# Two layers of a diffusion transformer block: the products of the identity ahead of two kinds of transposes are taken out

## The reference

```python
# layer 0
x_norm = modulate(_ln(x), shift_a, scale_a)
...
attn_w = jax.nn.softmax(jnp.einsum('bhqd,bhkd->bhqk', q, k) * scale, axis=-1)
attn_out = jnp.einsum('bhqk,bhkd->bhqd', attn_w, v)
...
x = x + gate_a[:, None] * attn_out
...
x = x + c_attn_out
...
x = x + gate_m[:, None] * h
# layer 1
x = res + sa
...
x = res + ca
...
x = res + (h @ ffn_w2.T + ffn_b2)
```

## Time and profile before

| | |
|---|---|
| time, median of 3 runs | 448.67 us (448.65 to 450.5) |
| profiled execution, from its first to its last instruction | 447.5 us |
| granted TensorE clock, mean over the span | 0.935 |
| PE busy | 399.2 us (89%) |
| DVE busy | 324.1 us (72%) |
| ACT busy | 263.9 us (59%) |
| POOL busy | 157.5 us (35%) |

### The profile page before, as it was taken

One profiled execution on the slowest core, in us unless ns is written; L12 is line 12 of the kernel. 1 busy time (PEld: TensorE's weight loads), 2 busy tenths in 40 slices (PEclk: granted clock), 3 DMA queues, 4 the chain that ended last, 5 costly groups with the idle time before them and its releaser, 6 DMA issues.

```text
span 447.5 us, 11248 instructions
## 1 busy us (share of the span) xinstructions
PE 399.2 (89%) x4368; PEld 256.7 (57%) x4368; DVE 324.1 (72%) x842; ACT 263.9 (59%) x521; POOL 157.5 (35%) x147
## 2 busy tenths in 40 slices
PE   1688989898988899999999999999999999989976
PEld 1445646464656654745646547556665665656754
DVE  6559686969687876794986977987999977381430
ACT  1414847464748585865756756537475667549642
POOL 6793384252615320251321602515526061011220
PEclk9965998969899999998998998969999989989999
DMA  7990030303030321030120120213030303000000
GB/s 233 278 351 7 2 144 3 145 3 140 3 141 3 139 91 51 4 144 3 48 97 4 47 97 4 97 51 115 27 112 30 141 3 139 26 3 4 25 25 23
DMA packets 18059, 33.58 MB, mean 75 GB/s; under 512 B 2527, under 2 KB 7135, under 8 KB 17759
## 3 DMA queue, kind: packets, MB, share of 16 engines
q1 hardware_dynamic: 16992, 28.85, 18.1%
q10 hardware_dynamic: 1015, 4.02, 3.0%
HBM read 6.51 MB, written 1.05 MB: 17 GB/s over the span
## 4 chain that ended last, share of the span: by engine, by line
PE 59%; DVE 22%; ACT 11%; issue 5%; ACTq 1%; DMA 1%; POOL 0%; DVEq 0%
DVE maxima L807 15%; PE ps_ao L1142 12%; PE ps_misc L1073 8%; PE ps_misc L1122 8%; ACT PT L989 7%; PE ps_misc L1171 6%; PE ps_misc L1193 5%; PE ps_misc L1098 4%; PE ps_misc L1022 4%; PE ps_misc L1178 3%; PE ps_misc L1083 3%; PE ps_misc L1027 2%; PE ps_misc L1151 2%; ACT xnT L974 2%; ACT L989 1%
## 5 line engine op out<-in xcount | busy, mean ns | idle before, releaser
L807 DVE TENSOR_REDUCE maxima<-ps_misc 128x4 f32<-128x512 f32 (+1 forms) x256 | 153.1, 663 | 21.9 <-PE ps_misc L1098 21.6
L989 ACT ACTIVATE PT<-ps_misc 128x512 f32<-128x512 f32 (+1 forms) x256 | 131.0, 607 | 30.2 <-PE ps_misc L1122 28.9
L887 POOL TENSOR_SCALAR Kd<-Kh,head_rows 128x512 fp32r<-128x512 f32 (+1 forms) x64 | 98.6, 1558 | 94.5 <-DVE maxima L807 69.5
L1142 PE MATMUL ps_ao<-PT,V 120*18 120x128 f32 (+1 forms) x2048 | 76.6, 296 | 5.1 <-ACT PT L989 4.4
L1142 PEld LDWEIGHTS ps_ao<-PT,V 120*18 120x18 f32 (+1 forms) x2048 | 55.2, 105 | 23.1 <-ACT PT L989 11.3
L1122 PE MATMUL ps_misc<-Qd,Ks 32*128 32x128 f32 (+1 forms) x1024 | 56.3, 293 | 10.0 <-ACT PT L989 4.6
L1122 PEld LDWEIGHTS ps_misc<-Qd,Ks 32*128 32x128 f32 (+1 forms) x1024 | 42.6, 191 | 34.6 <-issue 16.9
L868 POOL TENSOR_SCALAR vareps<-mv 128x4 f32<-128x4 f32 (+1 forms) x28 | 6.8, 243 | 149.9 <-DVE mv L700 149.3
L1098 PE MATMUL ps_misc<-Kd,Qh 32*128 32x512 f32 (+1 forms) x256 | 44.0, 528 | 1.0 <-DVE maxima L807 0.2
L852 DVE TENSOR_TENSOR x<-ps_misc,x 128x512 f32<-128x512 f32 x24 | 16.5, 689 | 38.6 <-PE ps_misc L1193 28.5
L1073 PE MATMUL ps_misc<-xnT,Wr 128*128 128x512 f32 x72 | 39.3, 668 | 4.7 <-ACT xnT L974 4.7
(11 more groups left out here) (80 smaller groups left out, 482.1 us busy)
## 6 DMA issues: line engine op xcount, KB each, us to landing
Qd<-Qh SPq DMA_DIRECT2D x32, 256.0 KB, 2.6
Ks<-Kh SPq DMA_DIRECT2D x16, 256.0 KB, 3.1
Qd<-Ql SPq DMA_DIRECT2D x16, 256.0 KB, 2.5
Ks<-Kh SPq DMA_DIRECT2D x16, 240.0 KB, 2.5
Ks<-Kl SPq DMA_DIRECT2D x8, 256.0 KB, 2.4
Ks<-Kl SPq DMA_DIRECT2D x8, 240.0 KB, 2.5
W<-weights ACTq DMA_DIRECT2D x1, 1792.0 KB, 15.6
x<-x_in SPq DMA_DIRECT2D x4, 256.0 KB, 6.9
```

What stands on the lines that cost most here:

```text
L807: dve.tensor_reduce(maxima[:, st.b // HB, st.b % HB, c, :], bank(st.use + c)[:, 0:NG * ns].rearrange("p (n k) -> p n k", n=NG), AX_X, ALU. ...
L887: pool.tensor_scalar(Kd[:, st.f % 2, st.h, 0:n], f32(Kh[:, st.f % 2, 0:n]), head_rows[:, st.h:st.h + 1], None, ALU.mult).then_inc(S["kd_re ...
L989: act.activation(PT[0:ns, st.k % PSLOTS, c, :, :].rearrange("p n t -> p (n t)"), bank(st.use + c)[0:ns, :], ACT.Exp, scale=SCALE).then_inc ...
L1142: last = pe.matmul(ps_ao[32 * c:32 * c + PAIR, block * P:(block + 1) * P], heads[:, at:at + PAIR], PT[0:ns, st.k % PSLOTS, c, n, :], start ...
```

## The change

The table `WARM` becomes empty, so that `warm` does nothing in any step. The order of all steps, all waits and all other instructions stay.

```diff
@@ -60,7 +60,7 @@
 PAIR = 2 * VW
 VSLOTS = 3
 PSLOTS = 3
-WARM = {"norm": 3, "aT": 3}
+WARM = {}
 
 
 WCOLS = {}
```

## The result

| | before | after |
|---|---|---|
| median | 448.81 us | 456.11 us |
| single runs | 448.65 to 450.5 (4) | 452.06, 455.41, 456.81, 460.4 |
| profiled execution's span | 447.5 us | 453.5 us |
| mean granted clock, profiled execution | 0.935 | 0.906 |

The ratio is 1.0128, 95% interval 1.0088 to 1.0168. The forecast was 453.0 us, 443 to 462, slower.

What follows compares the result with a forecast made beforehand. PE was taken to set the pace in most stages. A gain of 12.5 us and a clock loss of 16.8 us gave +4.3 us, 453.0 us against the median, range 443 to 462 us.

Steps and rivals of the forecast that it cites:

- The price of 1 us at 1.2 GHz: Read from three passes of attention 0: each 3.4 us at 1.2 GHz makes the kernel 1.4 us longer.
- the loss: Ten more clock falls, about 12 lengths of 3.4 us, 41 us more at 1.2 GHz, costing 16.8 us.
- The gain: Removing 48 products gives back 12.5 us, at 22 places on the chain; bounds about 8 and 16.6 us.
- the full places: 13 chain places where the copy has long landed; each gives its whole 0.65 or 0.75 us, 9.05 us together.
- the 22 places: Products on the chain of work that ended last: 13 give all, eight 0.34 to 0.55 us, one nothing.
- The ten places: Ten sparse stretches holding products at 2.4 GHz; without them PE keeps 2.48 us of work, so ten new falls.
- The clock didn't hold: Rival that the clock holds: fewer than seven lengths added, kernel faster, 443 us with five, 436 with none; 23%.
- The products weren't hidden: Rival that products only fill time lost to waits: 448.7 us and the same clock; no more than 2%.
- Transposes do hold the clock: Rival that transposes don't hold the clock: a fall at every second place, 24 lengths, 470 us; 5%.

Runs made afterwards that it cites:

- The kernel with the products off the chain kept: Against the kernel before, only 13 norm and 14 aT products stay, those off the chain or giving nothing; 444.2 to 456.2 us, mean 449.9.
- the quarter products: Against the kernel before, all 48 products keep 384 columns but use 32 rows of the identity in place of 128; 457.5 us.
- the six transposes: Against the kernel before, six transposes of the identity into the same bank replace the product at all 48 places; 448.1 us.
- the experiment with eleven products kept: Against the kernel before, products stay at only 11 of 48 places, those of the prediction's ten sparse stretches; 451.6 us.
- the 16 products of aT alone: Against the kernel before, products stay only ahead of the 16 aT, the 32 ahead of norm are out; 448.6 us.
- the 32 of norm: Against the kernel before, products stay only ahead of the 32 norm, the 16 ahead of aT are out; 452.0 us.

## Why the prediction was right

**The direction and the mechanism held.** Low clock went from 55.0 us in the mean of 79 runs to 92.3 us in four, 37 us more; the forecast was 41. (In the two profiled executions it is 34 us behind the first norm, and 27 us in all.) The price of 1 us at 1.2 GHz was set at 1.4 / 3.41 = 0.41 us; among the runs of one kernel, where the program is the same and the clock differs, it came out at 0.34 to 0.42 us in nine kernels of the table, 0.27 in two, and 0.30 in the kernel before. So the loss is 37 x 0.36 to 0.40 = 13 to 15 us, and 10 to 16 by the whole spread of slopes, where 16.8 was forecast. The nearness of PE to full work at 1.2 GHz (69.9 of 71.7 us) was the right reason to take the price near its upper end.

**The gain was too large.** It was put at 12.5 us, with 8 as the lower bound. The measured 7.3 us and a loss of 13 to 15 leave 6 to 8 us, and a loss of 10 to 16 leaves 3 to 9. The step that failed: that "the chain names PE, and no wait, at the full places". It does, but the next wait lay just behind. In the five passes with the same low clock before and after lie nine of the 22 places, 0.34 to 0.75 us each by the prediction's prices, and those passes are together no shorter than before (within 0.1 us). Ahead of the second product of layer 0's MLP it can be seen at work: at the three places ahead of L1178 in passes of attention 1, PE gave 0.43 us of 0.65 back to ACT's gelu (1.3 us in all), and what was left did not shorten the two of these passes that can be compared. The kernel with the products off the chain kept says the same without a slope: in its two runs at 54.9 us of low clock, 21 products of the chain are out at the clock of before, and the time is about 4 us under before's mean of 448.8, where 12.5 was forecast. Which wait took up the gain was read only ahead of L1178. Some gain there is: the pass from 275.26 to 312.52 us takes 36.51 in place of 37.26 us with 3.4 us more at 1.2 GHz.

Both terms were too large, so their errors partly cancelled: +4.3 forecast, +7.3 measured. That the sum came within about 3 us is in part luck.

An estimate at an equal clock agrees. Carried to 55 us at 1.2 GHz with 0.4 us each, the kernel without products would take 456.2 - 0.4 x 37.3 = 441.3 us, 7.5 less than before (6.0 less at 0.36 us each). By the same sum the quarter products stand at 457.5 - 7.6 = 449.9 and the six transposes at 448.1 + 0.7 = 448.8: whatever they compute, instructions of this length cost the same 7 to 9 us (6 to 8 at 0.36). And not all of it lies on the chain of before: the 27 products that the prediction put at nothing cost 1 to 4 us by this estimate (444.2 and 444.9 us with them, 441.3 to 442.8 without).

**The ten places were half right.** Seven falls are new in the profile after and one (208.9) is gone. Five of the seven follow one of the ten stretches: 75.0, 180.8, 317.4, 389.0 and 409.5. Two, at 344.7 and 440.2, are elsewhere. Of the other five stretches, the one at 287 us lies about where the old fall of 294 now begins, at 290; those of 97, 150, 389 and 420 us (in the times of before) stayed at 2.4 GHz. The count came out at ten lengths of 3.4 us in the profile (34.1 us more), where twelve were forecast; the list came out by half, and the experiment with eleven products kept shows why no such list is safe: with products there, six of the seven new falls stayed away in its profiled execution, but one came all the same, and two old ones grew.

**The rivals.** The clock didn't hold (mean 0.906, below the 0.92 named as the sign that it would). The products weren't hidden. Transposes do hold the clock (six of them).

What stays open is why the falls come in different places from run to run of one kernel, which spreads its times over 2%: 447.4 to 456.2 us with eleven kept, by 61.5 to 81.8 us at 1.2 GHz. The traces show when the clock changed, not what decides it. That the 16 products of aT alone hold the clock better than the 32 of norm is measured; why, no run shows.

## What to carry to other kernels

An instruction whose result nobody reads can earn its place: price it by what it costs where PE is behind, and by what the clock costs when it is gone, 0.27 to 0.42 us for each us at 1.2 GHz here. Put such work where PE waits for another engine in any case, not where it is behind; a few in the right steps beat many. And give a gain on the chain only up to the next wait: look one step past the removed work for what would be late then. The surest test of a gain is a stretch that has the same clock before and after.

## What the runs showed of the hardware that was not expected

A transpose of 128 x 128 fp32 is one record of 273 ns where a product is two; six transposes hold the clock as one product of 384 columns does (53.2 and 55.0 us low). A product over 32 rows takes as long as one over 128 (481 and 486 ns in the median; 536 and 513 in the mean, which holds what ran at 1.2 GHz) and holds the clock less. The time of one program on one core varies mostly with the clock's falls: within a kernel, the line through its runs tells the time of a run from its time at 1.2 GHz to within 2.5 us (behind the slopes of the changed kernels stand correlations of 0.81 to 0.97, in the kernel before 0.76).
